# The last four output projections of a cross-attention in split fp32r parts, and W2's second half loaded in two quarters

## The chip, the cores and the metric

The kernel runs on one core of a Trainium2 chip. The metric is the device time of one execution in microseconds (us); the kernel before has a median of 1299.98 us over three runs (1298.57 to 1300.05). Everything below is float32 in and float32 out.

## What is computed

```python
x = x + xattn(layernorm(x), ctx_1024)     # 16 x 64 latents of 256; contexts of 1024 rows; 16 heads of 64
x = x + linear_attention(layernorm(x))    # 2 x 512 rows in the module, 16 heads of 16, relu features of 64
x = x + moe(layernorm(x))                 # 8 experts, top 2, 256 -> 1024 -> 256

# xattn ends with:      out @ Wo + bo              out is [1024 rows, 1024], Wo is [1024, 256]
# the causal sums of the linear attention run over the 64 rows of a batch element
# moe: softmax of the two best of xn @ Wg; relu(xn @ W1[e] + b1[e]) @ W2[e] + b2[e]
```

## The kernel before

The 1024 rows are 8 tiles of 128 (TT = 8). The work has three stages. In the first, 128 steps (16 batches by 8 pairs of heads) compute the cross-attention; their outputs, transposed, gather in `qo` [128, 8 head pairs, 1024 rows], and Wo lies in `wo` [128, 8, 256].

In the second stage a loop over s = 0 to 7 runs on every engine, and the order of the work in each is written by hand. Step s does the linear attention of tile s and pieces of its neighbours. On TensorE it is, in this order: keys and queries (L1447), values (L1456), two transposes (L1496, L1513), the last three head pairs of the output projection of tile s+1 (`project_heads`, L1421), features (L1471), gate logits of tile s-2 (L1523), the linear attention's own projection of tile s-1 (L1507), head pairs 0 to 2 of the output projection of tile s+2, products (L1480), ranks (L1530, L1531), head pairs 3 and 4 of tile s+2, a transpose (L1430) and the weighted sum (L1490). A head pair is one matmul of 128x128 weights with 256 columns; in float32 the profile shows it as two matmul records. Tiles 0 to 3 are projected by the end of step 1, tiles 4 to 7 in steps 2 to 6.

VectorE in step s: the attention result of tile s-1 (L981 to L987), values with bias (L967), the residual and moments of tile s+1 (`projected`, L956, L942, L944), gating of tile s-2 (L999 to L1016), the residual of tile s-1 (L993), normalisations (L952), the mask of tile s (`masked`, L974, on which L1490 waits), slots (L1029 to L1035). ScalarE copies and activates what TensorE leaves in PSUM: L708, L720, L724, L732, the features L714, the gap L728, and `turned` (L697). GpSimd computes reciprocal deviations (L533, L535), adds a bias (L541) and scatters rows by indirect DMA (L552).

The third stage is the mixture of experts: 23 groups of 128 rows, three of them (EARLY = 3) before all rows are routed. For each, the rows come in (`rows_in`, L424), are turned (L1538, copied by VectorE at L1127), go through W1 (`hidden`, L1590) and W2 (`rows_out`, L1603, in float32 for the early groups; in fp32r parts, L1640 to L1642, for the others), and VectorE adds the weighted second bias (`second_bias` L1164, `weighted_rows` L1169). All eight experts' W2 stay in `w2_all`, 8 KB of a partition each. `rows_out(0)` waits until all four loads of W2 are there. On VectorE `second_bias(0)` waits for the load of all second biases, and `rows_turned(1)`, which feeds `hidden(1)`, stands behind it in the queue.

The fp32r parts of a float32 operand are a high one (a cast to fp32r on ScalarE) and a low one (operand less high part, on VectorE); three matmuls of parts (high by high, high by low, low by high) take the place of one in float32.

SyncE (SP) issues nearly all DMAs on one queue, in program order. Before, it issued all four W2 loads of 2 MB at the start of the second stage (L405), then the stores of tiles 0 to 5 (L409), the second bias (L416), W1 of group 0 (L420), the rows of groups 0 to 2 (L424), W1 of groups 1 and 2, and the last two stores.

Of the kernel before, what the change touches and what calls it, by code (L numbers as in the profile page):

```python
# [53 lines left out]
APAIRS = AH // 2  # L54
WB, XB = 3, 3


def build(nc, x, ctx_1024, cos, sin, lat_g, lat_b, ctx_g, ctx_b, Wq, Wkv, Wo, bo, Wqkv, bqkv, Wout, bout, proj,
          Wg, W1, b1, W2, b2, out):
    with ExitStack() as ctx:  # L60
# [68 lines left out]


        qo = sb("qo", [P, PAIRS, TOK], F32, xattn)
        xattn.close()
# [61 lines left out]
        group_expert = sb("group_expert", [P, GT], I32, lin)  # L194
        result_no = sb("result_no", [P, 2], U32, lin)
        w2_all = sb("w2_all", [P, E, FT, D], F32, lin)
        b2_all = sb("b2_all", [P, E, D], F32, lin)
# [129 lines left out]
        def _(sp):  # L327
# [82 lines left out]

            for e in range(0, E, 2):
                second_weights(e)
            for t in range(TT - 2):
                accumulate_from(t)
            sp.wait_ge(y_ps, TT)
            sp.dma_start(b2_all[:], b2.partition_broadcast(P)).then_inc(b2_ld, 16)  # L416

# [12 lines left out]
            for g in range(EARLY):  # L430
                rows_in(g)
            for g in range(1, EARLY):
                first_weights(g)
            for t in range(TT - 2, TT):
# [148 lines left out]
        def _(act):  # L583
# [146 lines left out]
            def second_rows(t):  # L730
                act.wait_ge(xn_done[1], t + 1)
                act.copy(xn_all[:, 1, t, 0:D], xn_all[:, 0, t, 0:D]).then_inc(second_done, 1)  # L732

            for s in range(TT):
                keys_queries(s)
                if 0 <= s - 1:
                    attention_turned(s - 1)
                if 0 <= s - 2:
                    input_turned(s - 2)
                    second_rows(s - 2)  # L740
                features(s)
                if 0 <= s - 2:
                    gap_turned(s - 2)
                if s + 1 < TT:
                    turned(s + 1)

            def bias_of(g):
# [50 lines left out]
        def _(dve):  # L798
# [326 lines left out]
            def rows_turned(g):  # L1125
                dve.wait_ge(xs_ps, g + 1)
                dve.tensor_copy(xsT[:, g % 2], xs_bank(g)[:, 0:D].rearrange("p (k c) -> p k c", k=KC)).then_inc(xsT_done, 1)  # L1127

            for s in range(TT):
                if 0 <= s - 1:  # L1130
# [4 lines left out]
                if 2 <= s <= TT - 2:  # L1135
                    projected(s + 1)
                if 0 <= s - 2:
                    gating(s - 2)
# [68 lines left out]
            def second_low(g):  # L1207
                e = expert_of(dve, g)
                if g == EARLY:
                    dve.wait_ge(w_ps, TT)  # L1210
                if g >= EARLY + 2:
                    dve.wait_ge(e_ps, g - 1)
                dve.wait_ge(part_hi_done, TT + g - EARLY + 1)
                dve.tensor_tensor(w2_lo[g % 2][:], w2_all[:, bass.ds(e, 1)].rearrange("p o f d -> p (o f) d"),
                                  w2_hi[g % 2][:].bitcast(F32), ALU.subtract).then_inc(part_lo_done, 1)
# [24 lines left out]
        def _(pe):  # L1240
# [173 lines left out]
            def project_heads(t, first, end):  # L1414
                if first == 0 and t == 0:
                    pe.wait_ge(ku_done, STEPS)
                    pe.wait_ge(wo_ld, 32)
                if first == 0 and t >= 3:
                    pe.wait_ge(y_done, t)
                for g in range(first, end):  # L1420
                    last = pe.matmul(y_bank(t), qo[:, g, t * P:(t + 1) * P], wo[:, g], start=(g == 0), stop=(g == PAIRS - 1))  # L1421
                if end == PAIRS:
                    last.then_inc(y_ps, 1)
# [207 lines left out]
            def rows_out_parts(g, first, end):  # L1631
                if first == 0:
                    pe.wait_ge(ys_done, g)
                    pe.wait_ge(part_lo_done, TT + g - EARLY + 1)
                    pe.wait_ge(h_split, 4 * (g - EARLY) + 2)
# [50 lines left out]
```

## Time and profile before

| | |
|---|---|
| median of 3 runs (lowest to highest) | 1299.98 us (1298.57 to 1300.05) |
| time of the profiled execution | 1297.51 us |
| its span, from the first to the last instruction | 1295.8 us |
| TensorE / VectorE / ScalarE / GpSimd busy | 98% / 76% / 48% / 47% of the span |
| mean granted clock of TensorE | 0.997 |
| second stage, step s = 0 to the first rows of group 0 | 1030 to 1122 us |
| early groups 0 to 2 | 1122 to 1151 us |
| first record of steps 3, 4 and 5 (L1447) | 1062.80, 1075.41, 1088.02 |
| end of the last projection (tile 7, L1421); issue of the second bias; issue of W1 of group 0 | 1105.28; 1109.42; 1115.41 |
| first use of W1 of group 2 by TensorE | 1143.66 |
| GpSimd's L533 and L535 behind L944 in step 3 | 0.19 us from 1068.68, 0.57 us from 1068.94 |
| granted clock in the windows of 1 us from 1123 to 1128 | 0.87, 0.50, 0.50, 0.50, 0.92 |

The profiled execution lies 1.06 us under the lowest and 2.47 us under the median of the timed runs. Times in the rows are counted from the start of the span. A row of the timeline gives the start, the length, the engine, the line, the operation, its operands and how many records are merged in it; a bracket says how long the engine had idled and who released it.

### The profile page before, as it was taken

How to read it: one execution, taken by the hardware profiler on the slowest of the kernel's cores; microseconds unless marked ns; L12 is line 12 of the kernel's file. 1: busy time of each engine (PE TensorE's matmuls, PEld its weight loads, DVE VectorE, ACT ScalarE, POOL GpSimd, SP SyncE). 2: the span in 40 equal slices, each digit the busy share in tenths (PEclk: the TensorE clock that was granted, in tenths of full speed). 3: DMA queues.
4: the chain of work that ended last, by engine and by line, in shares of the span. 5: the costliest groups of instructions: out<-in, count | busy, mean ns of one | idle time of the engine just before them, and what ended most of it. 6: DMA issues, size and time to landing. Idle time of an engine off the chain costs nothing.

```text
span 1295.8 us, 43930 instructions
## 1 busy us (share of the span) xinstructions
PE 1270.2 (98%) x18292; PEld 1138.5 (88%) x18292; DVE 982.3 (76%) x1973; ACT 621.7 (48%) x1264; POOL 608.7 (47%) x611
## 2 busy tenths in 40 slices
PE   7999999999999999999999999999999999999997
PEld 4788998899889989998998899889889888799997
DVE  7887787787778787877887788778766456668886
ACT  6345444544444454445444444544454333356664
POOL 3465554555455555544654555555433123333333
PEclk9999999999999999999999999999999999999999
DMA  6243343434343434343343434343444350556662
GB/s 221 58 122 85 102 115 84 110 75 119 82 108 77 121 79 107 81 118 81 104 118 84 108 75 121 80 108 79 114 115 107 97 209 31 181 177 193 197 199 50
DMA packets 71493, 145.56 MB, mean 112 GB/s; under 512 B 18232, under 2 KB 45568, under 8 KB 69120
## 3 DMA queue, kind: packets, MB, share of 16 engines
q1 hardware_dynamic: 67216, 138.53, 40.6%
q0 software_dynamic: 4080, 4.22, 1.6%
q8 instruction: 146, 2.39, 0.8%
q14 instruction: 51, 0.42, 0.1%
HBM read 61.74 MB, written 14.76 MB: 59 GB/s over the span
## 4 chain that ended last, share of the span: by engine, by line
PE 95%; DVE 2%; ACT 1%; issue 1%; DMA 1%; POOLq 0%; POOL 0%; SPq 0%; ACTq 0%; DVEq 0%
PE bank L1290 29%; PE bank L1324 10%; PE bank L1326 9%; PE bank L1325 9%; PE bank L1276 9%; PE bank L1590 7%; PE bank L1336 4%; PE bank L1306 2%; PE bank L1297 2%; PE bank L1421 2%; PE bank L1640 2%; PE bank L1642 1%; PE bank L1641 1%; PE bank L1447 1%; PE bank L1603 1%
## 5 line engine op out<-in xcount | busy, mean ns | idle before, releaser
L496 POOL TENSOR_TENSOR kr<-kr,ksw 128x1024 f32<-128x1024 f32 x128 | 318.5, 2489 | 451.9 <-DVE pr L854 329.0
L1324 PE MATMUL bank<-x_hi,p_hi 128*128 128x258 f32 x1024 | 300.8, 294 | 0.0
L1326 PE MATMUL bank<-x_hi,p_lo 128*128 128x258 f32 x1024 | 288.6, 282 | 0.0
L1325 PE MATMUL bank<-x_lo,p_hi 128*128 128x256 f32 x1024 | 287.8, 281 | 0.0
L1290 PE MATMUL bank<-ct_hi,wk_hi 128*128 128x512 f32 x512 | 213.5, 417 | 2.5 <-DVE kr L876 2.3
L869 DVE TENSOR_TENSOR kw<-bank,stab 128x1024 f32<-128x1024 f32 x128 | 156.7, 1224 | 61.5 <-PE bank L1290 61.4
L608 ACT COPY o_part<-bank 128x64 f32<-128x64 f32 x128 | 27.2, 213 | 363.8 <-PE bank L1336 363.8
L1290 PE MATMUL bank<-ct_hi,wk_lo 128*128 128x512 f32 x512 | 201.3, 393 | 0.0
L1290 PE MATMUL bank<-ct_lo,wk_hi 128*128 128x512 f32 x512 | 200.6, 392 | 0.0
L854 DVE TENSOR_SCALAR pr<-pr 128x1024 f32<-128x1024 f32 x128 | 90.2, 704 | 138.3 <-ACT pr L612 138.1
L1325 PEld LDWEIGHTS bank<-x_lo,p_hi 128*128 128x128 f32 x1024 | 194.7, 190 | 0.0
L1326 PEld LDWEIGHTS bank<-x_hi,p_lo 128*128 128x128 f32 x1024 | 193.6, 189 | 0.0
L1324 PEld LDWEIGHTS bank<-x_hi,p_hi 128*128 128x128 f32 x1024 | 193.2, 189 | 0.0
L612 ACT ACTIVATE pr<-bank 128x1024 f32<-128x1024 f32 x128 | 131.7, 1029 | 98.9 <-PE bank L1276 89.1
L887 DVE TENSOR_TENSOR p_lo<-pr,p_hi 128x1024 fp32r<-128x1024 f32 x128 | 159.7, 1247 | 2.2 <-ACT p_hi L628 2.2
L876 DVE TENSOR_TENSOR kr<-bank,ctab 128x1024 f32<-128x1024 f32 x128 | 152.7, 1193 | 0.0
L1276 PE MATMUL bank<-qs,kr 64*64 64x64 f32 x8192 | 142.6, 218 | 0.0
L628 ACT CAST p_hi<-pr 128x1024 fp32r<-128x1024 f32 x128 | 134.7, 1052 | 15.9 <-DVE pr L854 5.0
L1276 PEld LDWEIGHTS bank<-qs,kr 64*64 64x64 f32 x8192 | 131.8, 135 | 0.7 <-issue 0.5
L1290 PEld LDWEIGHTS bank<-ct_hi,wk_hi 128*128 128x128 f32 x512 | 95.9, 187 | 28.0 <-DVE kr L876 2.4
L1290 PEld LDWEIGHTS bank<-ct_hi,wk_lo 128*128 128x128 f32 x512 | 96.1, 188 | 21.1
L1290 PEld LDWEIGHTS bank<-ct_lo,wk_hi 128*128 128x128 f32 x512 | 96.3, 188 | 15.9
(220 smaller groups left out, 2187.2 us busy)
## 6 DMA issues: line engine op xcount, KB each, us to landing
ksw<-kw SPq DMA_DIRECT2D x512, 128.0 KB
raw<-in_ctx_dram SPq DMA_DIRECT2D x16, 1024.0 KB, 6.1
w_two<-in_L_ffn_W_dram SPq DMA_DIRECT2D x16, 1024.0 KB, 5.2
x_slots<-fill SPq DMA_DIRECT2D x128, 64.5 KB, 3.3
w_all<-in_L_ffn_W_dram SPq DMA_DIRECT2D x4, 2048.0 KB, 15.6
wo<-in_L_ffn_W_dram SPq DMA_DIRECT2D x7, 1024.0 KB, 4.9
xs<-x_slots SPq DMA_DIRECT2D x23, 129.0 KB, 2.1
raw<-in_x_dram SPq DMA_DIRECT2D x4, 512.0 KB, 4.4
```

Of the source, the lines that this page charges most:

```text
L496: pool.tensor_tensor(kr[:, i], kr[:, i], ksw[:, i], ALU.add).then_inc(kr_done, 1)
L612: act.activation(pr_by_head, heads, ACT.Exp, scale=SCALE).then_inc(exp_done, 1)
L628: act.copy(p_hi[:, i], pr[:]).then_inc(p_hi_done, 1)
L869: dve.tensor_tensor(kw[:, i], psK, stab[:], ALU.mult).then_inc(kw_done, 1)
L876: dve.tensor_tensor(kr[:, i], psK, ctab[:], ALU.mult).then_inc(ku_done, 1)
L887: dve.tensor_tensor(p_lo[:, i], pr[:], p_hi[:, i].bitcast(F32), ALU.subtract).then_inc(p_lo_done, 1)
L1276: last = pe.matmul(heads[c * N:(c + 1) * N, h, t], kr[rows, j % 2, at:at + N], qs[rows, b, g], start=True, stop=True)
L1290: last = pe.matmul(psK[:, cols], l[:, k, w], r[:, b, k, cols], start=(m == 0), stop=(m == len(parts) - 1))
L1324: pe.matmul(psZ[:, 0:D + 2], p_hi[:, i, c], x_hi[:, b, t], start=(t == 0), stop=False, skip_group_check=True)
L1325: pe.matmul(psZ[:, 0:D], p_hi[:, i, c], x_lo[:, b, t], start=False, stop=False, skip_group_check=True)
L1326: last = pe.matmul(psZ[:, 0:D + 2], p_lo[:, i, c], x_hi[:, b, t], start=False, stop=(t == ST - 1), skip_group_check=True)
L1590: last = pe.matmul(h_bank(g, f), w1[g % WB][:, k, f * P:(f + 1) * P], xsT[:, g % 2, k], start=(k == 0), stop=(k == KC - 1))
```

## The change

Four things are changed. (1) For tiles 4 to 7 (`FROM = 4`) `project_heads` issues three fp32r matmuls a head pair in place of one in float32. Their operands are made by two casts and two subtractions: `wo` once, 128x2048, the cast on ScalarE at the end of step 0 and the subtraction on VectorE in step 1; each tile's columns of `qo`, 128x1024, cast on ScalarE at the end of steps 1 to 4 and subtracted on VectorE in steps 2 to 5, between `projected` and `gating`. The low part is written over `qo` itself. TensorE waits for the low part before a tile's first head pair. (2) The high and low parts of Wo and the two buffers of the tile's high part take the room of experts 4 to 6 in `w2_all`, so W2's second half is loaded later: experts 4 and 5 once the last projection is done, before the store of tile 5 and W1 of group 0; experts 6 and 7 behind the rows of groups 0 to 2 and ahead of W1 of group 1. (3) The load of the second biases moves from before W1 of group 0 to between W1 of group 1 and W1 of group 2. (4) Counts of two semaphores shift by the new parts. `rows_out(0)` still waits for all four W2 loads.

```diff
--- before.py
+++ after.py
@@ -53,6 +53,9 @@
 CH = TOK // 2
 APAIRS = AH // 2
 WB, XB = 3, 3
+WO_PARTS = TT
+FROM = 4
+EXPERT_PARTS = WO_PARTS + 1 + TT - FROM
 
 
 def build(nc, x, ctx_1024, cos, sin, lat_g, lat_b, ctx_g, ctx_b, Wq, Wkv, Wo, bo, Wqkv, bqkv, Wout, bout, proj,
@@ -128,6 +131,8 @@
         xl = raw[:, 1]
 
 
+        with ExitStack() as low:
+            qo_lo = sb("qo_lo", [P, PAIRS, TOK], F32R, low)
         qo = sb("qo", [P, PAIRS, TOK], F32, xattn)
         xattn.close()
 
@@ -193,6 +198,11 @@
         group_f = sb("group_f", [P, GT], F32, lin)
         group_expert = sb("group_expert", [P, GT], I32, lin)
         result_no = sb("result_no", [P, 2], U32, lin)
+        with ExitStack() as middle:
+            sb("w2_first", [P, E // 2, FT, D], F32, middle)
+            wo_hi = sb("wo_hi", [P, PAIRS, D], F32R, middle)
+            wo_lo = sb("wo_lo", [P, PAIRS, D], F32R, middle)
+            qo_hi = sb("qo_hi", [P, 2, PAIRS, P], F32R, middle)
         w2_all = sb("w2_all", [P, E, FT, D], F32, lin)
         b2_all = sb("b2_all", [P, E, D], F32, lin)
         w1_two = sb("w1_two", [P, WB - 1, KC, F], F32, lin)
@@ -408,12 +418,13 @@
                 sp.wait_ge(x2_done, t + 1)
                 sp.dma_start(acc[t * P:(t + 1) * P, :], raw[:, 0, t]).then_inc(acc_st, 16)
 
-            for e in range(0, E, 2):
+            for e in range(0, E // 2, 2):
                 second_weights(e)
-            for t in range(TT - 2):
+            for t in range(TT - 3):
                 accumulate_from(t)
             sp.wait_ge(y_ps, TT)
-            sp.dma_start(b2_all[:], b2.partition_broadcast(P)).then_inc(b2_ld, 16)
+            second_weights(E // 2)
+            accumulate_from(TT - 3)
 
             def first_weights(g):
                 e = expert_of(sp, g)
@@ -429,8 +440,10 @@
             sp.wait_ge(scattered, 16 * TOPK * EARLY_TILES)
             for g in range(EARLY):
                 rows_in(g)
-            for g in range(1, EARLY):
-                first_weights(g)
+            second_weights(E // 2 + 2)
+            first_weights(1)
+            sp.dma_start(b2_all[:], b2.partition_broadcast(P)).then_inc(b2_ld, 16)
+            first_weights(2)
             for t in range(TT - 2, TT):
                 accumulate_from(t)
             sp.wait_ge(group_done, 3)
@@ -731,6 +744,16 @@
                 act.wait_ge(xn_done[1], t + 1)
                 act.copy(xn_all[:, 1, t, 0:D], xn_all[:, 0, t, 0:D]).then_inc(second_done, 1)
 
+            def output_weights_high():
+                act.wait_ge(z_ps, STEPS)
+                act.wait_ge(wo_ld, 32)
+                act.copy(wo_hi[:], wo[:]).then_inc(part_hi_done, 1)
+
+            def outputs_high(t):
+                if t >= FROM + 2:
+                    act.wait_ge(y_ps, t - 1)
+                act.copy(qo_hi[:, t % 2], qo[:, :, t * P:(t + 1) * P]).then_inc(part_hi_done, 1)
+
             for s in range(TT):
                 keys_queries(s)
                 if 0 <= s - 1:
@@ -743,6 +766,10 @@
                     gap_turned(s - 2)
                 if s + 1 < TT:
                     turned(s + 1)
+                if s == 0:
+                    output_weights_high()
+                if FROM <= s + 3 < TT:
+                    outputs_high(s + 3)
 
             def bias_of(g):
                 e = expert_of(act, g)
@@ -1126,6 +1153,15 @@
                 dve.wait_ge(xs_ps, g + 1)
                 dve.tensor_copy(xsT[:, g % 2], xs_bank(g)[:, 0:D].rearrange("p (k c) -> p k c", k=KC)).then_inc(xsT_done, 1)
 
+            def output_weights_low():
+                dve.wait_ge(part_hi_done, WO_PARTS + 1)
+                dve.tensor_tensor(wo_lo[:], wo[:], wo_hi[:].bitcast(F32), ALU.subtract).then_inc(part_lo_done, 1)
+
+            def outputs_low(t):
+                cols = slice(t * P, (t + 1) * P)
+                dve.wait_ge(part_hi_done, WO_PARTS + 1 + t - FROM + 1)
+                dve.tensor_tensor(qo_lo[:, :, cols], qo[:, :, cols], qo_hi[:, t % 2].bitcast(F32), ALU.subtract).then_inc(part_lo_done, 1)
+
             for s in range(TT):
                 if 0 <= s - 1:
                     result(s - 1)
@@ -1134,6 +1170,10 @@
                     early_rows()
                 if 2 <= s <= TT - 2:
                     projected(s + 1)
+                if s == 1:
+                    output_weights_low()
+                if FROM <= s + 2 < TT:
+                    outputs_low(s + 2)
                 if 0 <= s - 2:
                     gating(s - 2)
                 if 0 <= s - 1:
@@ -1210,7 +1250,7 @@
                     dve.wait_ge(w_ps, TT)
                 if g >= EARLY + 2:
                     dve.wait_ge(e_ps, g - 1)
-                dve.wait_ge(part_hi_done, TT + g - EARLY + 1)
+                dve.wait_ge(part_hi_done, EXPERT_PARTS + g - EARLY + 1)
                 dve.tensor_tensor(w2_lo[g % 2][:], w2_all[:, bass.ds(e, 1)].rearrange("p o f d -> p (o f) d"),
                                   w2_hi[g % 2][:].bitcast(F32), ALU.subtract).then_inc(part_lo_done, 1)
 
@@ -1417,8 +1457,16 @@
                     pe.wait_ge(wo_ld, 32)
                 if first == 0 and t >= 3:
                     pe.wait_ge(y_done, t)
+                if first == 0 and t >= FROM:
+                    pe.wait_ge(part_lo_done, WO_PARTS + 1 + t - FROM + 1)
                 for g in range(first, end):
-                    last = pe.matmul(y_bank(t), qo[:, g, t * P:(t + 1) * P], wo[:, g], start=(g == 0), stop=(g == PAIRS - 1))
+                    cols = slice(t * P, (t + 1) * P)
+                    if t < FROM:
+                        last = pe.matmul(y_bank(t), qo[:, g, cols], wo[:, g], start=(g == 0), stop=(g == PAIRS - 1))
+                    else:
+                        pe.matmul(y_bank(t), qo_hi[:, t % 2, g], wo_hi[:, g], start=(g == 0), stop=False)
+                        pe.matmul(y_bank(t), qo_hi[:, t % 2, g], wo_lo[:, g], start=False, stop=False)
+                        last = pe.matmul(y_bank(t), qo_lo[:, g, cols], wo_hi[:, g], start=False, stop=(g == PAIRS - 1))
                 if end == PAIRS:
                     last.then_inc(y_ps, 1)
 
@@ -1631,7 +1679,7 @@
             def rows_out_parts(g, first, end):
                 if first == 0:
                     pe.wait_ge(ys_done, g)
-                    pe.wait_ge(part_lo_done, TT + g - EARLY + 1)
+                    pe.wait_ge(part_lo_done, EXPERT_PARTS + g - EARLY + 1)
                     pe.wait_ge(h_split, 4 * (g - EARLY) + 2)
                 for f in range(first, end):
                     if f == FT // 2:
```

## Rows read from the trace of the kernel before

**Rows 1.** The chain that ended last, window 1080 to 1296, by line.

```profile
by line: PE bank L1590 39.1%; PE bank L1640 9.1%; PE bank L1642 8.8%; PE bank L1641 8.8%; PE bank L1603 5.0%; PE bank L1421 3.6%; PE bank L1538 2.5%; issue 2.3%; PE bank L1447 1.8%; PE bank L1471 1.5%; PE bank L1490 1.5%; DMA xs<-x_slots 1.
```

**Rows 2.** Timeline of TensorE (PE) in step 3, from the end of tile 4's projection.

```profile
1065.99 1.46 PE L1421 MATMUL bank<-wo,qo 128*128 128x256 f32 x6
1067.38 1.17 PE L1471 MATMUL bank<-qkT,feat_w 32*128 32x128 f32 x32
...
1070.05 1.56 PE L1421 MATMUL bank<-wo,qo 128*128 128x256 f32 x6
1071.54 1.16 PE L1480 MATMUL bank<-feat_q,feat_k 64*64 64x64 f32 x64
...
1073.10 1.11 PE L1421 MATMUL bank<-wo,qo 128*128 128x256 f32 x4
1074.04 0.38 PE L1430 MATMUL bank<-ident,xn 128*128 128x128 f32 x2
1074.36 1.13 PE L1490 MATMUL bank<-vbd,am 128*64 128x34 f32 x32
```

**Rows 3.** Timeline of TensorE: first and next after twelve fp32r matmuls of group 3.

```profile
1160.78 0.36 PE L1640 MATMUL bank<-w_hi,h_hi 128*128 128x256 f32 x1
...
1162.30 2.95 PE L1590 MATMUL bank<-xsT,wo 128*128 128x128 f32 x25
```

**Rows 4.** Timeline of VectorE (DVE) in step 3, after tile 4's projection.

```profile
1068.41 0.18 DVE L944 BATCH_NORM_AGGREGATE mom<-st 128x2 f32<-128x6 f32 x1
1069.14 0.17 DVE L999 COPY logit<-bank 128x8 f32<-128x8 f32 x1 [0.54 <-PE bank L1523]
...
1072.77 1.29 DVE L974 TENSOR_TENSOR am<-bank,mask 128x512 f32<-128x512 f32 x2 [0.55 <-PE bank L1480]
```

**Rows 5.** Line L887, with min/median/max in ns, and timelines of POOL and DVE beside it.

```profile
L887 DVE TENSOR_TENSOR p_lo<-pr,p_hi x128: 1208/1215/2467, 59.4 to 1017.8; 128x1024 fp32r<-128x1024 f32 x128
...
1008.51 2.36 POOL L496 TENSOR_TENSOR kr<-kr,ksw 128x1024 f32<-128x1024 f32 x1 [5.19 <-DVE pr L854]
...
1009.49 2.47 DVE L887 TENSOR_TENSOR p_lo<-pr,p_hi 128x1024 fp32r<-128x1024 f32 x1 [1.11 <-ACT p_hi L628]
```

**Rows 6.** Splits of 128x2048 (tile w_all), min/median/max in ns.

```profile
L767 ACT CAST w_hi<-w_all x20: 1899/1906/1909, 1149.4 to 1275.8; 128x2048 fp32r x20
L1214 DVE TENSOR_TENSOR w_lo<-w_all,w_hi x20: 2284/2293/2293, 1152.2 to 1279.2; 128x2048 fp32r<-128x2048 f32 x20
```

**Rows 7.** Idle time of ScalarE behind L697 (step 4), of VectorE in step 1.

```profile
1077.50 1.14 ACT L708 ACTIVATE qkT<-bank,vecs 128x128 f32<-128x128 f32 x4 [2.67 <-PE bank L1447]
...
1046.68 0.42 DVE L993 TENSOR_TENSOR raw<-bank,raw 128x256 f32<-128x256 f32 x1 [2.35 <-PE bank L1507]
```

**Rows 8.** Timeline of SP's queue: the three row loads of groups 0 to 2.

```profile
1118.45 2.55 SPq L424 DMA_DIRECT2D xs<-x_slots  x3
```

**Rows 9.** DMA issues with median us to landing: the first W2 load, and line L409's.

```profile
w_all<-in_L_ffn_W_dram SPq DMA_DIRECT2D x1, 2048.0 KB, 7.8
...
DMA to landing us min/median/max: 1.7/1.9/8.5
```

**Rows 10.** Windows of 1 us: busy per engine, then clock, DMA share, GB/s.

```profile
1051.00:1052.00 1.00, 1.00 (x22) 0.96 (x19) 0.43 (x2) 0.00 (x0) 0.00 (x0) 1.00 1.08 385
...
1125.00:1126.00 1.00, 1.00 (x7) 1.00 (x6) 0.00 (x0) 0.36 (x2) 0.69 (x2) 0.50 1.06 434
```

**Rows 11.** Timelines of TensorE and VectorE between groups 0 and 1.

```profile
1131.24 3.72 PE L1603 MATMUL bank<-w_all,raw 128*128 x16
...
1135.01 1.95 PE L1590 MATMUL bank<-xsT,w_two 128*128 128x128 f32 x16
...
1132.35 0.41 DVE L952 TENSOR_SCALAR xn_all<-raw,mom,rsd 128x256 f32<-128x256 f32 x1
1133.39 0.45 DVE L1164 TENSOR_SCALAR gb<-b_all,xs 128x256 f32 x1 [0.63 <-issue]
...
1133.82 0.41 DVE L1127 COPY xsT<-bank 128x256 f32<-128x256 f32 x1
```

## Prediction

> **What bounds the kernel now.** I read the page first, then the chain that ended last. TensorE is busy 98% of the span, and in the last two hundred microseconds the chain is nearly all TensorE lines [rows 1]. The projections (L1421) are 3.6% of that stretch. So a shorter projection is worth its whole length wherever TensorE goes straight on, and nothing where another engine is waited for. Hence the timelines of one step. In step 3 TensorE has no idle time: eight head pairs stand in three chunks of 6, 6 and 4 records, and from each chunk's first record to the next line's are 1.39 us (1065.99 to 1067.38), 1.49 (1070.05 to 1071.54) and 0.94 (1073.10 to 1074.04), 3.82 together [rows 2]. VectorE is the one close behind: `am` starts at 1072.77, ends 1.29 later at 1074.06, and TensorE starts the weighted sum that needs it at 1074.36 [rows 2, 4]. VectorE has 0.30 us in hand there and no more; that number decides how much of the gain is kept.
>
> The other view is SP's queue before the early groups, since three loads are moved there. The rows of groups 0 to 2 are issued from 1118.45 to 1121.00 [rows 8]; W2 is first needed at 1131.24; and between VectorE's L952, over at 1132.76, and the next use of the second bias at 1133.39 nothing but the register load lies (0.63 us) [rows 11].
>
> **The parts of fp32r on TensorE.** Twelve fp32r matmuls of the same shape take 1.52 us from the first to the next line (1160.78 to 1162.30), the first of them 0.20 and each other 0.12 [rows 3]. Nine, three head pairs, are 0.20 + 8 x 0.12 = 1.16 us, six are 0.80. The chunks save 1.39 - 1.16 = 0.23, 1.49 - 1.16 = 0.33 and 0.94 - 0.80 = 0.14, 0.70 us a tile. Over four tiles that would be 2.8; if the first matmul of a chunk costs 0.1 more behind other work, 0.4 a tile, 1.6.
>
> **The parts on ScalarE.** Wo's cast is 1.91 us [rows 6], behind `turned` at the end of step 0; a tile's cast has half the elements, some 0.95 to 1.05 us. Both stand where ScalarE idles 2.67 us in step 4 [rows 7] and in the first steps no less. Cost nothing; without that cover each would delay L708 and TensorE's features by its length.
>
> **The parts on VectorE.** Wo's subtraction is 2.29 us [rows 6], in step 1 ahead of the residual, where VectorE idles 2.35 [rows 7]: hidden with 0.06 to spare. A tile's subtraction has the form of L887, 1.215 us [rows 5]. It stands between `projected` and `gating`. In step 3 the aggregate ends at 1068.59 and gating starts at 1069.14: 0.54 us are free, and 1.215 + overlap of issue makes gating start 0.54 to 0.68 later. Masking started 0.55 after its predecessor because products came last [rows 4], so that too is absorbed: relative to the end of the projection's first chunk, `am` starts at about +5.3 (before: 1072.77 - 1067.38 = +5.39) and is ready at +6.6. TensorE, its two other chunks shorter by 0.47, could start the weighted sum at 1074.36 - 1067.38 - 0.47 = +6.51 and starts at +6.65 instead of +6.98. A step keeps 0.33 + 0.23 = 0.56 of the 0.70. TensorE itself comes to the tile's first head pair at 1070.05 - 1067.38 = +2.67, and the low part is there at +1.13 + 1.22 + 0.06 = +2.41: no wait.
>
> Step 2 differs: tile 3 is done already, so no first chunk is saved, and the residual, free of that wait, and the subtraction follow on values; I count its two chunks' gain as lost to `am`. Steps 3, 4 and 5 keep 0.56 each, step 6 has only the first chunk of tile 7, 0.23: 3 x 0.56 + 0.23 = **1.9 us**. From there to the first rows VectorE's counting and SP's loads set the pace and shift as a whole.
>
> One row speaks against it. While GpSimd ran an addition from 1008.51 to 1010.87, VectorE's subtraction of two operands from SBUF, begun at 1009.49, took 2.47 us, not 1.215, and ended 1.09 after GpSimd's end [rows 5]: it stood still until GpSimd was done. The new subtractions stand just where GpSimd computes the deviation of the same tile (it starts when L944 ends). The Trainium skill (SBUF — State Buffer, on the port pair that VectorE and GpSimd share) says that this pair is an exclusive lock held for a whole instruction, and that a VectorE instruction with two SBUF inputs contends for it with GpSimd's reads; the row agrees. If VectorE gets in first, GpSimd waits, which costs nothing, as normalisation comes three microseconds later; if GpSimd does, the subtraction starts up to its 0.76 us late (0.19 + 0.57, in the table). By the rule the gain of the loop would be 0.4 in the second case, 1.9 in the first; by the rows alone the bounds are the same 0.4 and 1.9, as the collision of rows 5 is the largest seen.
>
> **The moved loads.** Nothing waits for W2 in the second stage. Experts 4 and 5 are issued at about 1105.4, when the last projection is over, and 2 MB land 7.8 us after issue [rows 9], before W1 of group 0 is issued at 1115.4 (these two times stand in the table of the profile before). Cost nothing; the second bias that used those microseconds is gone from there.
>
> Experts 6 and 7 are issued at 1121.00, right behind the rows. 7.8 us later is 1128.8; the scatter of tile 5 (0.26 MB) runs beside it, so 1129.2. It is needed at 1131.24 [rows 11]: 2 us in hand. The queue is served in order (a 128 KB store behind two W1 loads took 8.5 us to land, alone 1.9 [rows 9]), so W1 of group 1 follows: at 385 GB/s [rows 10] 1 MB is 2.7 us, there at 1132, needed at 1135.01: hidden. Then the second bias, another 2.7, and the next scatter, 0.26 MB: 1134.2 to 1135.0; W1 of group 2 at 1137.7, needed at 1143.7.
>
> The second bias is late. VectorE would take it at 1132.76 and needs 0.63 + 0.38 + 0.05 + 0.41 until `xsT` of group 1 is ready; before it was ready at 1134.23, and TensorE came for it at 1135.01 [rows 11]. So 0.78 us of lateness are free, and no wait arises if the bias lands by 1133.5. At 1134.6 TensorE waits **1.1 us**. Bounds: nothing if the loads run at 434 GB/s, which the trace also shows [rows 10], and the bias lands at 1133.6; 3 us if each of the three loads takes 0.7 longer. All this shifts with the 1.9 us, loads and needs alike, so the sum stands. Behind VectorE's wait the numbers of the rows, `xsT` and the weighted rows queue, and TensorE waits for the second of these. The last two stores land at about 1138, so GpSimd's first addition comes 1 to 2 us later; its result is asked for ten microseconds on.
>
> **Sum.** The profiled execution's time was 1297.51, span 1295.8; -1.9 + 1.1 = -0.8 gives a span of 1295.0 and a time of 1296.7. It lies 2.47 below the median of the timed runs, so for the median 1299.98 - 0.8 = **1299.2 us**. 0.2%, 2.6 us, is about what can be told from no change.
>
> **Rivals.**
> 1. The gain is whole and the bias in time (chance 0.17). For it: 434 GB/s in rows 10, 0.78 us in hand, VectorE only 0.14 behind. Against it: one order of the queue, 5 MB behind 1121. Time 1299.98 - 1.9 = 1298.1, at most -2.8: 1297.2.
> 2. The subtraction and GpSimd collide, VectorE becomes the bound of steps 3 to 5 (0.2): the loop gains 0.4, the bias costs 1.1: 1300.7.
> 3. W2's last quarter comes after it is needed (0.13). It decides from a landing over 10.2 us after issue instead of 7.8, as with a rate that falls below some 260 GB/s while scatters and stores run too. Then `rows_out(0)` waits, and what is queued behind is late as well: a landing at 1133 costs 1.8, W1 of group 1 nothing more, the bias at 1138.5 costs 3.5 to 5 together; less 1.9 gives 1301.6 to 1303.1. Slower, against my forecast.
> 4. The clock. Before, it was granted at half, 1.2 GHz, around 1125 [rows 10] after the idle stretches of step 7. A wait of one microsecond more at 1135 could bring a second such stretch, of the same price: the windows from 1123 to 1128 lack 0.13 + 3 x 0.50 + 0.08 of full speed, 1.7 us; or the first may vanish, 1.7 won. 0.05 each way.
>
> The main case has the rest, 0.40, with 1298.4 to 1300.2 as its own range. Within 0.2% lie the main case, rival 2, most of rival 1, part of 3: 0.71. Faster by more than 0.2%: 0.12 (rival 1 at its end, or with the clock). Slower: 0.17 (rival 3, and 4 with 2). The range to hold the time 8 times in 10: 1297.0 to 1302.6.
>
> **What the profile after would show.** Chunks of nine fp32r matmuls in 1.16 us and of six in 0.80; steps 3 to 5 at 12.05 us instead of 12.61; `am` as what ends a wait of L1490 of some 0.1 us; `qo_lo` at 1.22 us, not 1.6 or more. Third quarter landed before W1 of group 0; the last landed about 8 us after issue; an idle TensorE of about 1 us before `hidden(1)`, with VectorE's L1164 late on a DMA. I am wrong if steps 3 to 5 stay at 12.6 us, if the subtraction in step 1 delays the residual and through it TensorE, or if `rows_out(0)` waits.

## The result, and the profile after

The changed kernel has a median of 1299.35 us over 12 runs (1298.16 to 1304.04), the kernel before on the same chips 1298.14 us over 12 (1295.37 to 1300.05). The ratio is 1.0023, 95% interval 1.0013 to 1.0033: about 3.0 us slower, where 0.8 us faster was forecast. The ratio is not the quotient of the medians, which lie 1.2 us (0.09%) apart; the means lie 2.2 us (0.17%) apart. That the median comes out beside the forecast's 1299.2 us is luck: the kernel before has 1298.14 in twelve runs and not the 1299.98 of three from which the forecast was counted. The profiled execution took 1299.40 us, its span is 1297.7.

The loop first: the timeline of TensorE in step 3 of the changed kernel, which answers to [rows 2]. L1467 to L1469 are the three fp32r matmuls of a head pair.

```profile
1064.46 2.05 PE L1495 MATMUL bank<-xnT,wqkvT 128*128 128x128 f32 x16
...
1067.57 0.36 PE L1467 MATMUL bank<-wo_hi,qo_hi 128*128 128x256 f32 x1
1067.77 0.28 PE L1468 MATMUL bank<-wo_lo,qo_hi 128*128 128x256 f32 x1
...
1068.81 1.17 PE L1519 MATMUL bank<-qkT,feat_w 32*128 32x128 f32 x32
...
1075.46 1.13 PE L1538 MATMUL bank<-vbd,am 128*64 128x34 f32 x32
1076.52 2.05 PE L1495 MATMUL bank<-xnT,wqkvT 128*128 128x128 f32 x16
```

Nine matmuls take 1.24 us (1067.57 to 1068.81), and the step 12.06 us (1064.46 to 1076.52) instead of 12.61. Steps 4 and 5 take 12.05 and 12.06. Beside it VectorE and GpSimd, against [rows 4]:

```profile
1069.84 0.18 DVE L971 BATCH_NORM_AGGREGATE mom<-st 128x2 f32<-128x6 f32 x1
1069.93 1.19 DVE L1163 TENSOR_TENSOR qo_lo<-qo,qo_hi 128x1024 fp32r<-128x1024 f32 x1
1071.05 0.16 DVE L1026 COPY logit<-bank 128x8 f32<-128x8 f32 x1
...
1070.10 1.08 POOL L546 TENSOR_TENSOR vpe<-mom,cvec 128x1 f32<-128x1 f32 x1 [1.44 <-DVE mom L971]
```

VectorE's subtraction got in first and took 1.19 us; it was GpSimd's first instruction that took 1.08 us, where it took 0.19 before. Nobody waited for it. The subtraction took 1.19 us in all four steps.

Then the other half: SP's queue at the start of the third stage, against [rows 8] and the issue times in the table of before.

```profile
1105.08 0.39 SPq L415 DMA_DIRECT2D w_all<-in_L_ffn_W_dram  x1
...
1115.20 0.26 SPq L431 DMA_DIRECT2D w_two<-in_L_ffn_W_dram  x1
1118.33 3.00 SPq L435 DMA_DIRECT2D xs<-x_slots  x3
1121.38 0.44 SPq L415 DMA_DIRECT2D w_all<-in_L_ffn_W_dram  x1
1122.56 1.48 SPq L431 DMA_DIRECT2D w_two<-in_L_ffn_W_dram  x1
1124.08 0.75 SPq L445 DMA_DIRECT2D b_all<-in_L_ffn_b_dram  x1
```

The DMA view, issue to landing in the last column, has the second bias:

```profile
b_all<-in_L_ffn_b_dram SPq DMA_DIRECT2D x1, 1024.0 KB, 12.2
```

It landed at 1136.3 (1124.08 + 12.2). The third quarter, issued at 1105.08, was in by 1113: there the traffic falls from 280 GB/s to 18. The timelines of TensorE and VectorE, against [rows 11], show what waited:

```profile
1122.42 0.66 PE L1586 MATMUL bank<-ident,xs 128*128 128x128 f32 x2 [1.73 <-DMA xs<-x_slots]
...
1133.33 3.72 PE L1651 MATMUL bank<-w_all,raw 128*128 x16
1136.89 0.38 PE L1561 MATMUL bank<-ident,xn_all 128*128 128x128 f32 x2
1138.19 2.02 PE L1638 MATMUL bank<-xsT,w_two 128*128 128x128 f32 x16 [0.92 <-issue]
...
1137.34 0.35 DVE L1204 TENSOR_SCALAR gb<-b_all,xs 128x256 f32 x1 [2.47 <-issue]
```

TensorE waited 1.73 us for the first rows (before 0.97 us) and 0.92 us before `hidden(1)` (L1638); VectorE stood 2.47 us before L1204, the reader of the bias. The forecast had 1.1 us for the wait before `hidden(1)`; that it comes within 0.2 us is luck, since landing and need were both later than forecast. The windows show one reason (busy of PE, PEld, DVE, ACT, POOL, then clock, DMA share, GB/s; to hold against [rows 10]):

```profile
1122.00:1123.00 1.00, 0.58 (x2) 0.29 (x2) 0.00 (x0) 0.00 (x0) 0.00 (x0) 0.56 0.96 191
...
1128.00:1129.00 1.00, 1.00 (x7) 1.00 (x6) 0.00 (x0) 0.31 (x2) 0.00 (x0) 0.53 1.13 412
```

From the wait for the rows to 1129 the granted clock is at its half level, 1.2 GHz: 0.44 + 5 x 0.50 + 0.47 = 3.4 us short of full speed, against 1.7 before. So `hidden(0)`, 8.1 us long before (to `rows_out(0)`), took 8.5 us, and `hidden(1)` was late for two reasons: the bias, and the half clock before it.

To compare kernels whose first stages differ by a microsecond or two, times are counted below from the first record of step 0 (1029.96 before, 1031.58 after), written with a plus sign. The first stage is the same work in both. It differs by its own stretches of half clock, at 12 to 19 and 60 to 64 us in the changed kernel's trace and absent in that of before; over all fourteen traces step 0 begins at 1029.7 to 1030.3 in the six without half clock there, and at 1031.0 to 1031.9 in the eight with it. Before: first rows turned +91.75, `hidden(0)` +93.15, `hidden(1)` +105.05. After: +90.84, +93.29, +106.61. The loop's end was 1.85 us earlier, the rows 0.9; `hidden(0)` was 0.14 later, `hidden(1)` 1.56 later.

Behind that the changed kernel won something that nobody had forecast. From the first use of W1 of group 2 to the end of the span it takes 150.55 us, the kernel before 152.14. TensorE's longest wait there, before and after:

```profile
1279.36 0.36 PE L1640 MATMUL bank<-w_hi,h_hi 128*128 128x256 f32 x1 [1.91 <-issue]
```

```profile
1282.78 0.36 PE L1688 MATMUL bank<-w_hi,h_hi 128*128 128x256 f32 x1 [1.55 <-issue]
```

Before, a stretch of half clock follows, 1.7 us short of full speed:

```profile
1282.00:1283.00 1.00, 1.00 (x6) 1.00 (x6) 0.81 (x2) 0.00 (x0) 0.00 (x0) 0.50 0.00 0
```

All three traces with float32 projections (before, e1, e8) have the wait of 1.91 us and this stretch, and take 152.1 to 153.2 us from there to the end. All eleven with the parts wait 1.44 to 1.56 us, have no half clock there before TensorE's last matmul and take 150.5 to 151.7. Why the wait is shorter is not shown; the change touches only counts of semaphores there.

### The profile page after: what moved, and what is told of

It reads as the page before. It is cut to its first block, busy times and chain, and to the rows that moved or that the text cites. A ratio compares the mean times of both kernels' runs of the same rounds, so it can differ in the third digit from the quotient of the medians.

```text
span 1297.7 us, 44009 instructions
## 1 busy us (share of the span) xinstructions
PE 1270.5 (98%) x18324; PEld 1140.0 (88%) x18324; DVE 988.6 (76%) x1978; ACT 627.9 (48%) x1269; POOL 609.9 (47%) x611
## 4 chain that ended last, share of the span: by engine, by line
PE 95%; DVE 2%; issue 1%; DMA 1%; ACT 1%; POOL 0%; POOLq 0%; SPq 0%; ACTq 0%; DVEq 0%
PE bank L1330 29%; PE bank L1364 10%; PE bank L1366 9%; PE bank L1365 9%; PE bank L1316 9%; PE bank L1638 7%; PE bank L1376 4%; PE bank L1346 2%; PE bank L1337 2%; PE bank L1688 1%; PE bank L1689 1%; PE bank L1690 1%; PE bank L1396 1%; PE bank L1495 1%; PE bank L1465 1%; PE bank L1651 1%
```

## The experiments

Ratios are to the kernel before on the same chip; 0.1% is 1.3 us, and an interval of about 0.1% to each side stands on each, about 0.13% on the difference of two of them. The theory was that the loop keeps its 1.9 us and the moved loads take more than that back, through the bias above all; its rivals, that the parts cost elsewhere, or that the half clock is the cause and not a companion.

**e1, the loads without the parts.** Before, with the order of loads of the changed kernel.

```diff
-            for e in range(0, E, 2):
+            for e in range(0, E // 2, 2):
                 second_weights(e)
...
             sp.wait_ge(y_ps, TT)
-            sp.dma_start(b2_all[:], ...)
+            second_weights(E // 2)
...
+            second_weights(E // 2 + 2)
+            first_weights(1)
+            sp.dma_start(b2_all[:], ...)
+            first_weights(2)
```

> The kernel before with the loads of the change alone: W2's third quarter after the last projection, the fourth behind the rows of groups 0 to 2, the second bias between W1 of groups 1 and 2; all projections in float32. Theory A (the loads eat the gain of the parts): the loop's 1.9 us is absent and the cost of the loads is all there: TensorE idle before hidden(1) 1 us or more with L1164 late on the second bias, and 3 to 5 us slower than the kernel before. Theory B (the parts themselves cost time somewhere outside the loop, the loads nothing): equal to the kernel before within 1 us.

Measured: 1303.52 us, ratio 1.0053 (1.0039 to 1.0067), 6.9 us slower. The loads alone lose more than both halves together; the parts win some 0.30% of it back, 3.9 us and not the loop's 1.9: the rest fits what the parts win near the end. Its TensorE timeline has both waits:

```profile
1132.92 5.40 PE L1606 MATMUL bank<-w_all,raw 128*128 x16 [2.04 <-DMA w_all<-in_L_ffn_W_dram]
1140.13 2.02 PE L1593 MATMUL bank<-xsT,w_two 128*128 128x128 f32 x16 [1.59 <-issue]
```

The last quarter, issued at 1122.25, was waited for until 1132.9, 10.7 us later; then the bias was waited for.

**e2, the bias early.** The changed kernel with the bias back ahead of W1 of group 0.

```diff
             accumulate_from(TT - 3)
+            sp.dma_start(b2_all[:], ...)
...
             first_weights(1)
-            sp.dma_start(b2_all[:], ...)
             first_weights(2)
```

> The changed kernel with the load of the second biases put back ahead of W1 of group 0, behind the store of tile 5; the last quarter of W2 stays behind the rows. Theory A1 (the bias is what is late): no idle TensorE before hidden(1), 1.1 to 1.9 us faster than the changed kernel. Theory A2 (the last quarter's traffic, and with it the late rows of group 0 and the halved clock, is what costs): the first rows still land 4 us after issue, the clock is at half for two stretches of 3.3 us, and only the wait of 0.9 us before hidden(1) goes.

Measured: ratio 1.0004 (0.9995 to 1.0013). Against the changed kernel the bias's place costs 0.19%, 2.5 us (0.8 to 4.2 by the interval).

**e3, everything ahead of the rows.** Expert 7 loaded at the start (its room is free), experts 4 to 6 in one load after the last projection, then the bias; nothing behind the rows.

> The changed kernel with no W2 and no bias load behind the rows of group 0: expert 7 is loaded with the first half at the start of the stage, experts 4 to 6 in one load after the last projection, then the second biases, all ahead of W1 of group 0 (about 11 us of traffic in front of it). Theory A: the loads' cost is gone and the loop's gain stays: 1.5 to 2.5 us faster than the kernel before. Theory B (the parts cost time outside the loop): no faster than the changed kernel. If W1 of group 0 is late for the traffic in front of it, hidden(0) starts later than 2 us after the first rows are turned.

Measured: ratio 1.0018 (1.0009 to 1.0027). A miss: to have no load behind the rows gained nothing, since the rows themselves came late and a second stretch of half clock, at 1124 to 1128, followed the one at 1110. SP waited longer for the scatter and issued them at +89.43, where the changed kernel has +86.75, and e5 and e6 below, with the half clock in the same place as e3, +88.2.

**e4, the clock held.** Four fp32 matmuls that nothing uses (128x128 by 256 columns) in the changed kernel, one behind the last transpose of step 6, three at the end of step 7.

```diff
+            def idle_matmuls(n):
+                for _ in range(n):
+                    pe.matmul(bank[:, 3, D:2 * D], ident[:], wqkvT[:, 0, 0:D], start=True, stop=True)
```

> The changed kernel with four float32 matmuls of 128x128 by 256 more (their result is not used) where TensorE idles: one after the last transpose of step 6, three at the end of step 7 before the rows of group 0 are waited for. Theory C (the halved clock behind the idle stretch is where the time went): the granted clock stays at 1.00 from 1120 to 1130 and the kernel is 2 to 3 us faster than the changed kernel. If the clock is no part of the loss, 0 to 0.5 us slower than the changed kernel.

Measured: ratio 1.0027 (1.0015 to 1.0039), no gain. Full clock from 1104 to 1136 and `rows_out(0)` at +99.53, 2.2 us earlier than in the changed kernel, but both waits are longer:

```profile
1129.87 3.72 PE L1658 MATMUL bank<-w_all,raw 128*128 x16 [0.83 <-DMA w_all<-in_L_ffn_W_dram]
1136.84 3.04 PE L1645 MATMUL bank<-xsT,w_two 128*128 128x128 f32 x16 [3.03 <-issue]
```

The wait for the bias grew to 3.03 us, and half clock came behind it, at 1137. The half clock at 1122 is not what makes the changed kernel slow: without it the bias sets `hidden(1)`, at +106.50 against +106.61.

**e5, the parts without the late loads.** Experts 4 to 6 aren't loaded, the bias is early. `second_weights_of(e, n)`, here and below, loads n experts from e on.

> The parts with as good as none of the moved loads: experts 4 to 6 of W2 are not loaded at all, expert 7 comes with the first half, the second biases stand where they stood before, and every product with W2 takes expert 0's matrix, so the output is not the reference's. Theory A (the parts gain what the loop shows, the loads lose it): about 1.9 us faster than the kernel before, up to 3 if the clock holds. Theory B (the parts cost something outside the loop): no faster than the kernel before.

Measured: 1295.01 us, ratio 0.9976 (0.9966 to 0.9987). The whole gain of the loop is there: `hidden(0)` +92.86, `rows_out(0)` +99.36, `hidden(1)` +103.11, the last 1.94 us earlier than before, with one stretch of half clock of 1.7 us in each trace. By the timed runs it is 3.1 us (1.7 to 4.4), more than the 1.9, as the stretch near the end is gone too. Against e5 the moved loads of the changed kernel cost 0.47%, 6.1 us (4.4 to 7.8), where 1.1 was forecast.

**e6 and e7, one megabyte behind the rows.** Expert 7 at the start, 4 and 5 after the last projection, the bias ahead of W1 of group 0, expert 6 alone behind the rows; e7 has the four unused matmuls too.

```diff
+            second_weights_of(E - 1, 1)      # at the start
...
-            second_weights(E // 2 + 2)
+            second_weights_of(E - 2, 1)
```

> The changed kernel with 1 MB instead of 3 MB behind the rows and ahead of or between the W1 loads: expert 7 is loaded with the first half, experts 4 and 5 after the last projection, then the second biases ahead of W1 of group 0, and expert 6 alone behind the rows. If the volume behind the rows is what costs: faster than the version with 2 MB there (which stood 0.4 us above the kernel before), at 0.5 to 1.5 us faster than the kernel before. If it is any traffic at all there, or the late first rows, equal to that version.

> The same with the four unused matmuls in the idle time of TensorE (one behind the last transpose of step 6, three at the end of step 7). With the bias early nothing waits any more behind the early groups' first part, so the clock that is kept should now reach the end: hidden(0) 1.5 to 2 us earlier behind the first rows, and 1.5 to 2.5 us faster than the same kernel without them, about 3 us faster than the kernel before. If the clock falls somewhere later instead, no difference.

Measured: 0.9998 (0.9989 to 1.0007) and 0.9985 (0.9976 to 0.9994). e7 is the one version with all of the work that beats the kernel before; the 0.13% between e6 and e7 are no more than the interval of that difference.

**e8, before with the unused matmuls.**

> The kernel before with the same four unused matmuls. In its trace the clock was at half for 3.3 us around 1125, which is 1.7 us of work: 1 to 1.7 us faster than the kernel before if they keep the clock, equal or up to 0.4 us slower if they do not.

Measured: 0.9997 (0.9988 to 1.0006). Its trace has full clock from 1104 to 1152 too; `hidden(1)` is at +104.13, 0.9 us earlier than in the trace of before. By the timed runs that is worth nothing measurable.

**e9 and e10, what the quarters cost with the bias early.** e9 is e2 with the unused matmuls; e10 is e2 without the last quarter.

> The version with the second bias back ahead of W1 of group 0 (ratio 1.0004), and with four unused fp32 matmuls of 128x128 by 256 columns in the idle stretches of TensorE at the end of steps 6 and 7, which took the half-clock stretch at 1110 to 1114 away where one MB stood behind the rows and gave 0.13%. Theory A (what the quarters still cost, 0.28% over the version without them, is mostly the half-clock stretch, which with 2 MB behind the rows is some 7 us long): the stretch vanishes and the ratio is 0.9980 to 0.9990. Theory B (it is the rows landing 4 us after issue and the queue behind them; the clock is bystander): hidden(0) starts where it did, W1 of group 1 or the last quarter is waited for, and the ratio stays at 1.0000 to 1.0006.

> The version with the bias early, without the last quarter: experts 6 and 7 are not loaded, and every product with W2 takes expert 0's matrix, so the output is not the reference's; experts 4 and 5 are still loaded after the last projection, ahead of W1 of group 0, and then the bias. It splits the 0.28% between the version with both quarters late (1.0004) and the one with neither (0.9976). If the load behind the rows is what costs (it runs beside the rows, the scatter and W1 of group 1), the ratio is 0.9976 to 0.9984, as without either. If the third quarter ahead of W1 of group 0 costs (it pushes W1 and the rows back in the queue, so that TensorE idles longer and the clock falls), the ratio is 0.9996 to 1.0004. If both share it, 0.9990.

Measured: e9 0.9996 (0.9987 to 1.0005), e10 0.9993 (0.9984 to 1.0003). Between e2 and e5 lie 0.28%; taking the last quarter away gives 0.11% of it, and 0.17% is left with what stands ahead of the rows. With 0.13% to each side the first may be nothing, and the two can't be told apart. The first rows in e10 and in e5:

```profile
1122.85 0.66 PE L1585 MATMUL bank<-ident,xs 128*128 128x128 f32 x2 [2.36 <-DMA xs<-x_slots]
```

```profile
1120.75 0.41 PE L1588 MATMUL bank<-ident,xs 128*128 128x128 f32 x2 [0.22 <-DMA xs<-x_slots]
```

In e10 TensorE idled 2.36 us for them, the clock was at half from there to 1129, and `hidden(0)` took 8.4 us; in e5 0.22 us, and 6.5.

**e11, a megabyte less ahead of the late bias, and e12, the changed kernel again.** e11 is the changed kernel with expert 7 loaded at the start and expert 6 alone behind the rows; the bias stays late.

> The changed kernel (1.0023) with one thing else: expert 7 is loaded at the start of the second stage, so that only expert 6, 1 MB, stands behind the rows; the bias stays behind W1 of group 1. In the three versions so far that had expert 7 at the start, the profile shows the half-clock stretch at 1110 to 1114, where TensorE waits for others anyway, and full clock from 1116 on; in the three with four loads of a quarter it is at 1122 to 1129, in front of hidden(0). Theory A (the place of the stretch belongs to the order of loads): it is at 1110 to 1114 here too, hidden(0) to rows_out(0) takes 6.6 us instead of 8.5; but the bias still lands at 1134 to 1135 and holds hidden(1) for the rest; ratio 1.0010 to 1.0018. Theory B (the place is chance, one profile each): it is as likely at 1122 to 1129, and the ratio is 1.0010 to 1.0018 by the queue alone, the megabyte less.

> The changed kernel once more, for its profile. If the place of the half-clock stretch belongs to the kernel it is at 1122 to 1129 again, the rows of group 0 are waited for 1.7 us, the bias lands about 12 us after issue and hidden(1) starts 106.6 us behind step 0. If the place is chance it may be at 1110 to 1114, and then hidden(0) to rows_out(0) takes 6.6 us and the bias alone holds hidden(1), at the same 106.5.

Measured: e11 0.9999 (0.9990 to 1.0008), better than either theory had it. Its bias, issued at 1122.49, landed 10.0 us later at +100.9, and VectorE took it up at +104.05 without a wait for it. Beside e6, the same loads with the bias early (0.9998), its late place costs nothing here. The stretch of half clock was at 1122 to 1129, so the theory that the order of loads gives it its place fell. (Of the three kernels with expert 7 at the start that the expectation counts, e3 had a second stretch, at 1124.) e12 settles that: the same kernel, and the stretch is somewhere else. Its TensorE and VectorE timelines:

```profile
1109.69 1.93 PE L1538 MATMUL bank<-vbd,am 128*64 128x34 f32 x32 [0.74 <-DVE am L1001]
...
1129.81 3.72 PE L1651 MATMUL bank<-w_all,raw 128*128 x16 [0.29 <-DMA w_all<-in_L_ffn_W_dram]
...
1138.13 3.75 PE L1638 MATMUL bank<-xsT,w_two 128*128 128x128 f32 x16 [4.39 <-issue]
...
1137.28 0.35 DVE L1204 TENSOR_SCALAR gb<-b_all,xs 128x256 f32 x1 [6.20 <-issue]
```

and of its windows one from each of its two stretches of half clock:

```profile
1110.00:1111.00 1.00, 1.00 (x24) 1.00 (x23) 0.90 (x6) 0.00 (x0) 0.02 (x1) 0.50 1.08 382
...
1139.00:1140.00 1.00, 1.00 (x7) 1.00 (x7) 0.00 (x0) 0.00 (x0) 0.00 (x0) 0.50 0.04 15
```

Here the clock fell at 1110, in the loop's last steps; `hidden(0)` ran at full speed (+92.85 to +99.72, 6.9 us) and TensorE then stood 4.39 us for the bias, and at the end of that wait, at 1137, the clock fell to half again. `hidden(1)` began at +108.04. This execution took 1301.88 us, the other 1299.40; of the 12 timed runs eight lie from 1298.2 to 1300.0 and four from 1301.4 to 1304.0, which would fit the two ways to go, but the timed runs show no place of the stretch.

## Why the prediction was wrong

**Right.** The loop: 1.9 us forecast, 1.85 measured at the end of tile 7's projection, 1.94 still there at `hidden(1)` once the late loads are gone (e5). Two terms of it were off and cancel, which is luck. The chunks save 0.15 + 0.23 + 0.14 = 0.52 us a tile, not 0.70: a chunk of nine takes 1.24 to 1.26 us, 0.08 to 0.10 over the forecast, as the next line's start lies 0.2 behind the last matmul. But the first fp32r matmul starts 0.07 us earlier behind the transposes, and `am` took only 0.06, so a step keeps 0.55 where 0.56 was forecast. The subtraction took 1.19 us for 1.22. The third quarter had landed by 1113, before W1 of group 0 was issued. What the parts win near the end of the kernel had no term in the sum. Rival 2 did not happen: VectorE and GpSimd met in each of the four steps, and each time it was GpSimd, the later by 0.17 us, that waited. The Trainium skill (SBUF — State Buffer, "SBUF: two separate sides") has the port pair held for a whole instruction by whichever of the two starts first; GpSimd's 1.08 us beside VectorE's 1.19 agrees.

**The step that failed** is "all this shifts with the 1.9 us, loads and needs alike, so the sum stands", together with the price that hangs on it: 1.1 us for the bias and nothing for the quarters, where the timed runs have 6.1 us for both (e5 against the changed kernel). Where `hidden(0)` runs at full clock the need did shift: VectorE takes up the bias at +101.63 in e5, 1.8 before the +103.43 of before. In the changed kernel's profiled execution not even that: VectorE was free at +103.29 and with the 0.63 us of the register load would have taken it up at +103.9. The landing shifted in no execution. Forecast, shifted, it was 1134.6 - 1029.96 - 1.9 = +102.7; measured, +104.7 (1124.08 + 12.2 - 1031.58), in e4 +104.6 and in e12 +106.1 (1123.33 + 12.9 - 1030.09). Where the 2.0 and 3.4 us are:

- The last quarter, forecast at +89.1 (1121.00 - 1029.96 - 1.9), was issued at +89.80, 0.7 later: the rows were issued at +86.75, as forecast (88.49 - 1.9 = 86.6), but their three issues took 3.00 us and not 2.55. In e12, whose step 7 was late behind the half clock, the rows went out at +88.20 and the quarter at +90.80, 1.7 later.
- From the issue of the last quarter to the landing of the bias it took 14.9 us (1121.38 to 1136.3) and 15.3 in e12, not 13.6: the other 1.3 and 1.7. SP's own issue of W1 of group 1 took 1.48 us, where that of group 0 took 0.26, and the last quarter needed 8.9 us in e12 (1120.89 to 1129.8), 9.8 in e4 and 10.7 in e1, not 7.8. The 7.8 us came from a load at the head of the queue; here, behind three row loads and beside a scatter and two stores, no load of 2 MB was as quick.
- The last part of a load comes late. The trace counts a load's landing in 16 parts: of the bias's, fifteen were there at 1135.38 and the last at 1136.30, and in e12, e4 and e1 the last came 1.0 to 1.3 us behind the fifteenth. What holds it is not shown.
- From the landing to `hidden(1)` it took 1.89 us in all four executions in which the bias was waited for, where the forecast's four terms make 1.47: L1204 starts 1.04 us behind the landing, and not 0.63.

So the wait is 3.0 to 4.4 us where `hidden(0)` runs at full clock (e4, e12), with half clock at its end or behind it, and 0.9 where that stretch has already gone into `hidden(0)`. The timed runs put the bias's place at 2.5 us (e2) and find its cost gone with a megabyte less ahead of it (e11 against e6).

**The quarters.** Even with the bias in time the timed runs show no gain (e2, e6, e10, e11: 0.9993 to 1.0004). I had no term for the wait for the first rows, having let everything "from there to the first rows" shift as a whole: TensorE comes to them 1.7 us earlier, but takes them up 4.1 us after their issue in the changed kernel, 4.3 and 4.0 in e2 and e10, and 3.3 before. In every trace in which TensorE waited for them it could start no sooner than +90.7, whatever the time of issue. In the changed kernel fifteen of the first row load's 16 parts had landed at 1120.85, and the last at 1122.28, 0.14 before TensorE started; in e12 and e5 the last came 0.2 and 0.3 us behind the fifteenth. That it is the third quarter which makes the last part late was not shown.

What the traces do show goes with the place of the half clock:

| | half clock between 1100 and 1150 | first rows turned | `hidden(1)` | timed ratio |
|---|---|---|---|---|
| before | 1123 to 1128 | +91.75 | +105.05 | 1 |
| changed, bias late | 1122 to 1129 | +90.84 | +106.61 | 1.0023 |
| changed again, e12 | 1109 to 1114, 1137 to 1144 | +90.57 | +108.04 | |
| e2, bias early | 1120 to 1128 | +91.46 | +105.81 | 1.0004 |
| e10, e2 less the last quarter | 1122 to 1129 | +91.32 | +105.92 | 0.9993 |
| e11, 1 MB less ahead of the late bias | 1122 to 1129 | +90.83 | +105.83 | 0.9999 |
| e3, all loads ahead of the rows | 1110 to 1114, 1124 to 1128 | +91.99 | +105.52 | 1.0018 |
| e6, bias early, 1 MB behind the rows | 1110 to 1114 | +90.87 | +103.21 | 0.9998 |
| e5, no late loads | 1109 to 1114 | +90.70 | +103.11 | 0.9976 |
| e7 and e9, unused matmuls | none | +91.58, +91.54 | +103.35, +103.41 | 0.9985, 0.9996 |

With the bias in time, `hidden(1)` is at +105.5 to +105.9 where half clock falls on the first rows or on `hidden(0)`, and at +103.1 to +103.4, the loop's whole gain, where it stands at 1110 or is absent. So in the traces of e6, e7 and e9 the quarters take nothing from `hidden(1)`, while the timed runs of e6 and e9 are no faster than the kernel before. One trace a kernel doesn't say how often the timed runs went either way. So 0.28% of the 0.47% that the moved loads cost has no cause shown. Of rival 4, given 0.05, the size was right in the first execution (3.4 us short of full speed against 1.7), the place not: it came ahead of `hidden(0)`, and at 1137, behind the wait for the bias, only in e12 and e4.

**Rival 3** was half right: the last quarter was waited for in three executions (0.29, 0.83, 2.04 us), and with the kernel's own parts always under the 1.8 us that I priced. Its cost lay behind it, in the queue: the same megabytes that made it late made the bias later.

## What to carry to other kernels

When a gain of TensorE is set against a load moved back in a queue, don't shift the landing with the gain: work out each landing from its own issue, with all that the queue carries, and each need from the work; their difference is the wait. Order the queue by when each load is first read and by what stands behind its reader: here 1 MB of bias read by an instruction ahead of `xsT` in VectorE's queue cost 0.19% by its place, and nothing once a megabyte less stood ahead of it. And read the wait from an execution at full clock, for a stretch of half clock can hide it. Nor is one execution enough to price a change of 0.2%: two traces of the same kernel put `hidden(1)` 1.4 us apart here.

## What was not expected of the hardware

- A wait for a scatter grew with the loads beside it. SP waits for it before the row loads: 0.9 us in e5, with the 1 MB of bias issued after the last projection, 1.1 in the changed kernel, with 2 MB, 2.2 to 2.7 in e2, e6 and e10, with 3, and 4.7 in e3, with 4. In e3 the row loads were issued 5.8 us after W1 of group 0; in e5, with half clock at 1110 as well, 4.6 (1118.26 - 1113.69), where SP waited 2.6 us more for VectorE's `group_at` and not for the scatter. SP's timeline in e3:

```profile
1114.80 0.28 SPq L436 DMA_DIRECT2D w_two<-in_L_ffn_W_dram  x1
1120.61 2.59 SPq L440 DMA_DIRECT2D xs<-x_slots  x3
```

- The same 1 MB of bias took 12.1 to 12.9 us to land behind 3 MB and three row loads, 10.0 with 2 MB in place of the 3 (e11), and 7.7 behind the third quarter and a store (e2). Its last sixteenth came up to 1.3 us behind the others.
- The clock's stretch of half speed comes in one of two places of the same kernel, at 1110 or at 1122, in two executions with the same instructions; with four unused fp32 matmuls, of some 0.5 us each, it is absent from 1104 to 1152 in e7, e8 and e9, and in e4, where the late bias is waited for, it comes at 1137.
